# Products without a use on TensorE between the second layer's expansions and the transposes in front of its experts

## The reference, cut to what matters

```python
x = x + tanh(g_xattn[1]) * align(ctx, layernorm(x))      # expanded[j] = sum of ctx rows i on the path at j
xn = layernorm(x)                                         # "x4" in the kernel
logits = einsum('bld,ed->ble', xn, gate_weight)           # 8 experts
kth = sort(logits.reshape(-1))[4 * 128 * 6 - 1]
gates = logits * (logits >= kth)
h = gelu(einsum('bld,ehd->bleh', xn, w1) + b1)
y = einsum('bleh,edh->blde', h, w2) + b2
x = x + tanh(g_ffn[1]) * einsum('blde,ble->bld', y, gates)
```

## Time and profile before

| | |
|---|---|
| median of 3 runs | 749.88 us (748.67 to 750.19) |
| the profiled execution, whole | 751.28 us |
| its span, first to last instruction | 749.5 us |
| mean granted TensorE clock | 0.863 of full |
| TensorE busy | 577.0 us, 77% of the span |
| VectorE busy | 567.8 us, 76% |
| ScalarE busy | 409.5 us, 55% |
| GpSimd busy | 127.8 us, 17% |
| chain that ended last | TensorE 63%, VectorE 25%, ScalarE 8% |

### The profile page before, as it was taken

The page is one execution under the profiler, slowest core; times in us unless marked ns, Lnnn a source line. Parts: engine busy times, 40 slices in busy tenths (PEclk is TensorE's granted clock), DMA queues, the critical chain, the costliest instruction groups (busy, mean ns, idle before and its releaser), DMA issues.

```text
span 749.5 us, 17177 instructions
## 1 busy us (share of the span) xinstructions
PE 577.0 (77%) x6419; PEld 405.2 (54%) x6419; DVE 567.8 (76%) x1722; ACT 409.5 (55%) x782; POOL 127.8 (17%) x160
## 2 busy tenths in 40 slices
PE   1748998815345840065589999999999999999997
PEld 1423444402134640054577777777777777677776
DVE  5757788899969539998893565677787878787775
ACT  1746885678578342255534656566454544545452
POOL 3000344413100000000036777710000000000000
PEclk9968998955566985568656999999999999999999
DMA  7200000000010000022000000000000000010000
GB/s 206 59 1 1 3 3 2 2 1 0 1 56 2 1 3 0 0 83 88 0 1 1 1 2 2 2 1 2 15 2 3 15 0 14 0 42 0 15 1 16
DMA packets 19676, 12.14 MB, mean 16 GB/s; under 512 B 1148, under 2 KB 18456, under 8 KB 19608
## 3 DMA queue, kind: packets, MB, share of 16 engines
q1 hardware_dynamic: 19608, 11.25, 5.4%
HBM read 9.15 MB, written 2.10 MB: 15 GB/s over the span
## 4 chain that ended last, share of the span: by engine, by line
PE 63%; DVE 25%; ACT 8%; issue 2%; DMA 1%; SPq 1%; DVEq 0%
PE PS L1598 8%; PE PS L1600 8%; PE PS L1599 8%; PE PS L1582 7%; PE PS L1583 7%; PE PS L1584 7%; DVE A L1121 3%; PE PS L1405 3%; DVE Bm L1092 3%; PE PS L1415 2%; ACT Bm L589 2%; DVE hmm L1012 2%; DVE hmm L1013 2%; PE PS L1511 1%; PE PS L1424 1%
## 5 line engine op out<-in xcount | busy, mean ns | idle before, releaser
L672 ACT ACTIVATE A<-PS,small_t 128x512 f32<-128x512 f32 x256 | 168.4, 688 | 119.7 <-PE PS L1584 118.2
L1598 PE MATMUL PS<-kT_w,A 128*128 128x128 bf16 x1024 | 174.8, 219 | 0.0
L1599 PE MATMUL PS<-kT_w,A 128*128 128x128 bf16 x1024 | 174.8, 219 | 0.0
L1600 PE MATMUL PS<-kT_w,A 128*128 128x128 bf16 x1024 | 174.7, 219 | 0.0
L1223 DVE TENSOR_TENSOR A<-A 128x512 bf16<-128x512 f32 x192 | 123.3, 691 | 7.9 <-ACT A L672 6.7
L1599 PEld LDWEIGHTS PS<-kT_w,A 128*128 128x128 bf16 x1024 | 100.2, 98 | 7.4
L1598 PEld LDWEIGHTS PS<-kT_w,A 128*128 128x128 bf16 x1024 | 100.2, 98 | 7.5
L1600 PEld LDWEIGHTS PS<-kT_w,A 128*128 128x128 bf16 x1024 | 100.2, 98 | 0.0
L1583 PE MATMUL PS<-A,xn_w 128*128 128x512 bf16 (+1 forms) x256 | 98.0, 383 | 0.0
L1584 PE MATMUL PS<-A,xn_w 128*128 128x512 bf16 (+1 forms) x256 | 98.0, 383 | 0.0
L1582 PE MATMUL PS<-A,xn_w 128*128 128x512 bf16 (+1 forms) x256 | 97.9, 382 | 0.0
(11 more groups left out here) (325 smaller groups left out, 1154.3 us busy)
## 6 DMA issues: line engine op xcount, KB each, us to landing
slab<-in_L_ffn_w_dram SPq DMA_DIRECT2D x16, 256.0 KB, 2.9
xs<-in_x_dram SPq DMA_DIRECT2D x4, 512.0 KB, 7.0
cs<-in_ctx_dram SPq DMA_DIRECT2D x4, 512.0 KB, 7.3
out_dram<-xs SPq DMA_DIRECT2D x8, 256.0 KB, 2.3
Bm<-in_L_ffn_W_dram SPq DMA_DIRECT2D x2, 256.0 KB, 2.9
b2blk<-in_L_ffn_b_dram SPq DMA_DIRECT2D x12, 4.0 KB
onw_b<-n_L_xattn_outnorm_w_dram SPq DMA_DIRECT2D x1, 64.0 KB
ab_b<-in_L_ffn_b_dram SPq DMA_DIRECT2D x1, 64.0 KB
```

The source lines that it names most:

```text
L672: act.activation(hf[:, e % 2, c, :], bank(c), ACT.Gelu_apprx_tanh, bias=b1).then_inc(S["h_gelu"], 1)
L1598: pe.matmul(o, hh[:, e % 2, c, t], w2h[:, e, c, :], start=(c == 0 and k == 0), stop=False, skip_group_check=True)
L1599: pe.matmul(o, hh[:, e % 2, c, t], w2l[:, e, c, :], start=False, stop=False, skip_group_check=True)
L1600: ins = pe.matmul(o, hl[:, e % 2, c, t], w2h[:, e, c, :], start=False, stop=(c == NC - 1), skip_group_check=True)
```

## The change

`keep_warm` is called in three more places of TensorE's stream, always with bank 0: two products after the expansions of each of the groups 4 to 7, eight more after the last of them, and two after the transposes of each of the eight groups, ahead of the logits of the group before. That makes 8 + 8 + 16 = 32 products of 512 columns. They wait for nothing and signal nothing; no other engine's stream changes.

```diff
                     ins = pe.matmul(bank(1 + g % 2, P * k, P * k + P), path[:, b, :], cs[:, b, :], start=True, stop=True)
                 ins.then_inc(S["expanded"], 1)
+                if g >= 4:
+                    keep_warm(0, 2)
+            keep_warm(0, 8)
             pe.wait_ge(S["w_split"], 2 * E)
             for g in range(G4 + 1):
                 if g < G4:
...
                         ins = pe.matmul(bank(3, E * b, E * b + E), x4f[:, (g - 1) % 2, P * k:P * k + P], small_t[:, 84:92], start=True, stop=True)
                     ins.then_inc(S["logits_done"], 1)
+                if g < G4:
+                    keep_warm(0, 2)
```

## The result

The changed kernel takes 751.84 us (median of 15 runs, 749.46 to 753.63), the kernel before, beside it, 749.58 us (15 runs). The ratio is 1.0032, 95% interval 1.0022 to 1.0043: slower by 2.3 us, where 3.3 were forecast. The profiled execution has a span of 750.2 us and took 751.96 as a whole.

The account below looks back on a forecast made before the run. No single engine was taken to bound it everywhere; TensorE holds the chain from 389.01 us, apart from one counting round. All terms were 0 but +3.3 us, giving 753.2 us against the median of 749.88; range 750.8 to 755.5.

Parts of the forecast that it names:

- step 5: Pairs after the transposes of groups 4 to 7, where TensorE is the chain: four at 0.82 us, +3.3 us.
- step 6: Start of the experts: an earlier clock rise could save 1.4 us, a later one cost 0.3; taken as 0.
- step 7: GpSimd's splits against VectorE's normalisations: missing them up to -1.8 us, hitting others up to about +1; taken as 0.
- 1.: Pairs after the expansions of groups 4 to 7: TensorE's pauses cover all but the last pair; cost 0.
- 3.: Pairs after groups 0 to 3: four take 1.7 us at full clock, before VectorE's second half is there; cost 0.
- 2.: Eight more products, ten in a row with the last pair, behind the last expansions: 2.2 us of room, cost 0.
- Rival C: Clock doesn't rise under the ten products, so VectorE waits for ScalarE's copies: +5.5 us, 755.4 us; chance 0.12.
- 4.: Before group 4 TensorE has nothing to do for 3 us or more, so group 4 starts at half clock.
- rival A: Clock full from 389 us on, groups 1.67 us each and the first expert shorter: -5.6, 744.3 us; chance 0.10.

## Why the prediction was right

The direction, the mechanism and the size hold: 751.84 lies in the range, 1.4 us under the point. In the first profile the steps come to +2.9 (step 5), -0.9 (step 6) and -0.2 (step 7), together +1.8, against +2.3 between the medians. Step by step:

1. and 3. (pairs in the expansions and in groups 0 to 3, cost 0): right. Without the late pairs the ratio is 1.0009, at most 1.0023. What the pairs among the expansions do for the clock was not in the prediction. In all seven profiles that have them the clock is full at the last expansion (in two of them it fell at 365 to 366 us and came back by 370); in all four that lack them it had fallen by then.

2. (the ten, cost 0): the cost is right, the work given to them is not shown. They raised nothing here, since the clock was full already, and took 2.32 us; no other profile shows them raising it either, and no run leaves them out alone. ScalarE's copies of group 2 ended near 382.4 and the root ran at 385.15, 0.2 us earlier in its execution than before when the shift of 1.0 us is taken off. Rival C needed transposes that start after 379.3 with a clock at half; they started at 377.56, or 378.6 with the 1.0 us put back.

4. (the gap): right, and the heart of it. A pause of 3.59 us was expected as "3 us or more". That the pause is the cause, and not the transposes, is shown by the kernel with the pause filled: the same groups, the same pairs, clock at 1.00. The clock was at half when group 4 began or within 0.1 us of it in all four profiles with this pause of 3.6 us behind a full clock, and full in all three with the pause filled behind a full clock. One reading in step 4 was wrong: the 2.19 us pause had no full-clock work behind it, since the expansions after it took 2.08 us, as at half clock, and 1.16 before it. Nor does the length of a pause settle it below 3.6 us. With nothing ahead of the sixteen, the clock held through a pause of 2.19 us and fell in one of 1.35; in three other profiles it fell in one of 1.05 us or within 0.4 us behind it.

5. (four pairs at 0.82): mechanism right, the term a little large. Each group grew by 0.76 to 0.81 us, the last by 0.6, 2.9 in all from 11.5 to 14.5 against 3.3 forecast. A pair itself takes 0.81 us (390.26 to 391.07), as costed; but what follows it is a little shorter than it was: transposes to logits 0.86 us in place of 0.90, the last logits 1.5 in place of 1.7. I had not taken that off. In the trace the next group's first weight load (390.65 to 390.88) lies under the second product, which may be why; no run tests it.

6. (start of the experts, taken as 0): a chance of the execution. It gave back 0.9 us in the first profile (7.6 us in place of 8.5) and nothing in the second, and so accounts for the +1.9 and +2.9 us of the table above. The 2.4 us that the prediction took for the sixteen of layer 0 was read too short: TensorE had been at work since 53.12 us, 2.2 us ahead of them, and sixteen that began at half clock later needed 4.9 and 5.5 us until the clock rose. The two comparisons of the changed kernel with that before, 2.3 and 3.7 us, lie on both sides of the 3.3. How many of the fifteen runs of the first had the early rise is not known, so the agreement with 3.3 may be partly luck.

7. (VectorE against GpSimd, taken as 0): -0.2. The third split began at 382.48 and ran beside the statistics, not L715, which took 0.19 us where it sat on the chain for 0.48. The eight statistics took 1.56 us beside the split, as they did before, where a split ran beside the last 0.7 us of them; L715 took 0.47 to 0.50 us in the four profiles in which a split ran beside it, and 0.19 in the seven others. The add had ended at 382.44, before the split began. That splits can miss the normalisations altogether, worth 1.9 us of VectorE's time, came up only in the kernel with the ten, the pause and the late pairs.

The rival A was no fancy: its sum of -5.6 us, for a full clock from 389 on, is what the filled pause gave, -6.2. The table load that it counts took 1.28 us on ScalarE before (L672, from 402.07). Its condition was missing from the change, not its mechanism. Where I was wrong is in how little the late products can do: I had taken that a clock at half stays there; with four a group it rose within group 7 (0.51 up to 402.2, 0.95 from there). For two a group, which is what the change has, it stayed in all three profiles.

How far transposes hold a full clock, the runs show in part. Groups of transposes and narrow logits alone lost it in two experiments, at 382.7 us (ten, pause and late pairs) and at 394.5 (pause filled, no late pairs), though with waits of 0.74 and 1.70 us among them, and none separates transposes from logits. But transposes do run at a full clock where it is there: four take 0.60 us in the filled-pause kernel at 1.00, against 1.06 to 1.12 at 0.50.

## What to carry to other kernels

Here the products that turned the loss into a gain stood in a pause of TensorE, the 3.59 us ahead of group 4; a pair in the stretch that TensorE itself bounded was paid nearly in full, 0.6 to 0.8 us each at half clock. Look for the longest pause ahead of the bound stretch. In this kernel, with that one left empty, the products before it earned nothing; with it filled, those products and the ones inside the stretch were worth 2.5 and about 5 us (from +2.3 to -6.2 us with one number changed). Take the length of the pause as it will be at full clock: this one was 2.01 us behind groups 0 to 3 at half clock and 3.59 behind them at full.

## What the runs showed that was not expected

Four products per group raised a clock at half before the experts began, in the one execution that was profiled, though they cost 3.3 us more than two; the median came out level with before (0.9990).

The runs of a kernel can lie far apart: 5.4 us with one late product and 7.9 with four, against 1.15 us with the pause filled and the pairs in place. In both wide ones a profile shows the clock changing level within groups 4 to 7 or as they end, so the spread may come from when it does. It is no sure sign, though: the runs of the kernel before spread over 6.2 us, and the changed kernel's over 4.2 us in fifteen runs and 0.6 in six. A small spread does not mean a full clock either, since those six had it at half in the groups.
